# A recurrent attention kernel gets a new order of its slots: scores three slots and values four slots behind the projection, LayerNorm and FFN spread over more slots

## The reference

```python
xn = layernorm(x)
s = linear_attention_and_convolution(xn)                    # once
y = xn
for layer in range(6):
    q, k, v = split(shift(y) @ Wqkv)          # 16 heads of 64, 1024 columns each
    q = rotary(l2norm(q) * qs); k = rotary(l2norm(k) * ksc)
    sim = q @ k.T * 8      # each window of 32 tokens sees itself and the window before
    y = softmax(mask(sim)) @ v @ Wo + y
    a, gate = split(layernorm(shift(y)) @ W1 + b1)          # 341 columns each
    y = (a * gelu(gate)) @ W2 + b2 + y
out = x + s * silu(y)
```

## Time and profile before

| | us |
|---|---|
| median of 3 runs | 1839.14 (1838.91 to 1840.05) |
| the profiled execution, its own time | 1847.78 |
| its span, first to last instruction | 1846.0 |
| TensorE busy | 1697.0 (92%) |
| VectorE busy | 1422.5 (77%) |
| ScalarE busy | 1343.9 (73%) |
| GpSimd busy | 1307.7 (71%) |
| the 16 transfer engines, share of their span | 11.9% |

### The profile page before, as it was taken

One profiled execution on the slowest core, in us unless ns is written; L12 is line 12 of the kernel. 1 busy time (PEld: TensorE's weight loads), 2 busy tenths in 40 slices (PEclk: granted clock), 3 DMA queues, 4 the chain that ended last, 5 costly groups with the idle time before them and its releaser, 6 DMA issues.

```text
span 1846.0 us, 68784 instructions
## 1 busy us (share of the span) xinstructions
PE 1697.0 (92%) x26160; PEld 1292.7 (70%) x26160; DVE 1422.5 (77%) x3011; ACT 1343.9 (73%) x2663; POOL 1307.7 (71%) x1305
## 2 busy tenths in 40 slices
PE   6889999999999999999999999999999999999984
PEld 5667777777677777767777777777777777677763
DVE  4488777787887778788777777878778787787763
ACT  3367777777777777777777777777777777777764
POOL 5187777777777777777777777777777777776654
PEclk8799999999999999999999999999999999999986
DMA  5011101011110111111011111111101001100000
GB/s 161 10 36 40 32 28 34 29 41 43 35 30 28 34 40 42 35 31 30 28 46 41 33 34 28 30 34 48 37 28 34 28 26 41 36 26 24 26 21 23
DMA packets 41407, 66.14 MB, mean 36 GB/s; under 512 B 7072, under 2 KB 16032, under 8 KB 41376
## 3 DMA queue, kind: packets, MB, share of 16 engines
q1 hardware_dynamic: 40224, 65.38, 11.9%
q10 hardware_dynamic: 1152, 0.34, 0.1%
HBM read 20.61 MB, written 1.05 MB: 12 GB/s over the span
## 4 chain that ended last, share of the span: by engine, by line
PE 69%; ACT 11%; issue 10%; DVE 8%; POOL 2%; ACTq 1%; DMA 0%; POOLq 0%; DVEq 0%
PE ps_a L536 11%; PE ps_qs L536 10%; PE ps_f L536 10%; PE ps_po L536 8%; PE ps_q L536 7%; PE ps_k L536 5%; PE ps_v L536 5%; PE ps_po L651 4%; PE ps_qs L642 3%; PE ps_tk L642 3%; DVE ssq L1273 2%; ACT p_bd L940 2%; DVE prob L1310 2%; ACT L1008 2%; ACT squares L946 2%
## 5 line engine op out<-in xcount | busy, mean ns | idle before, releaser
L425 POOL TENSOR_TENSOR qk<-qk,rnorm 128x512 f32<-128x512 f32 x384 | 393.2, 1045 | 298.5 <-DVE rnorm L1300 298.5
L417 POOL TENSOR_TENSOR qk<-qk,qk_rot 128x512 f32<-128x512 f32 x384 | 483.8, 1276 | 118.0 <-DVE qk_rot L1267 118.0
L1273 DVE TENSOR_REDUCE ssq<-squares 128x8 f32<-128x512 f32 x384 | 257.9, 681 | 71.0 <-ACT squares L946 58.1
L940 ACT COPY p_bd<-ps_po 64x512 f32<-64x512 f32 x380 | 219.0, 576 | 24.9 <-PE ps_po L651 22.5
L432 POOL TENSOR_TENSOR prob<-prob,row_inv 128x512 f32<-128x512 f32 x192 | 200.2, 1043 | 41.8 <-DVE row_inv L1319 41.8
L1316 DVE TENSOR_REDUCE row_sum<-prob 128x8 f32<-128x512 f32 x192 | 131.7, 686 | 119.8 <-ACT prob L1047 119.2
L536 PEld LDWEIGHTS ps_qs<-k_t,q_t 64*32 64x32 f32 x12224 | 178.8, 107 | 56.9 <-issue 56.9
L536 PE MATMUL ps_qs<-k_t,q_t 64*32 64x64 f32 x12224 | 209.7, 218 | 0.0
L1047 ACT ACTIVATE prob<-prob 128x512 f32<-128x512 f32 x190 | 120.0, 632 | 110.3 <-DVE prob L1310 107.0
L536 PEld LDWEIGHTS ps_po<-p_bd,v_back 128*64 128x64 f32 x3056 | 162.4, 138 | 48.0 <-issue 31.5
L536 PE MATMUL ps_po<-p_bd,v_back 128*64 128x64 f32 x3056 | 193.4, 225 | 1.1 <-ACT p_bd L940 1.0
(11 more groups left out here) (231 smaller groups left out, 4102.3 us busy)
## 6 DMA issues: line engine op xcount, KB each, us to landing
v_back<-v_own SPq DMA_DIRECT2D x192, 192.0 KB, 2.4
w_raw<-in_wqkv SPq DMA_DIRECT2D x48, 192.0 KB, 2.3
v_back<-v_own SPq DMA_DIRECT2D x96, 64.0 KB, 2.1
wo_sb<-in_wo SPq DMA_DIRECT2D x12, 256.0 KB, 3.1
w_sb<-in_w SPq DMA_DIRECT2D x6, 341.0 KB, 3.4
w_sb<-in_w SPq DMA_DIRECT2D x6, 192.0 KB, 2.6
x_in<-in_x SPq DMA_DIRECT2D x4, 256.0 KB, 5.2
out<-s_out SPq DMA_DIRECT2D x8, 128.0 KB, 1.9
```

The source lines that it names most:

```text
L417: nc.gpsimd.tensor_tensor(qk[:, s, i, :], qk[:, s, i, :], qk_rot[:, s, i, :], ALU.add).then_inc(added, 1)
L425: nc.gpsimd.tensor_tensor(heads(qk[:, s, i, :]), heads(qk[:, s, i, :]), rnorm[:, s, 8 * i:8 * i + 8].unsqueeze(2).to_broadcast([P, 8, HEAD ...
L940: return nc.scalar.copy(o, i)
L1273: V.tensor_reduce(ssq[:, s, 8 * i:8 * i + 8], heads(squares[:, s, OCTET * i:OCTET * i + OCTET]), AX, ALU.add).then_inc(ssq_done, 1)
```

## The change

A slot is put in a new order on every engine, and the stages are moved apart. TensorE now does: q projection of `u`, scores of `u-3`, transpose of the probabilities of `u-4`, k and v projections of `u`, both transposes of `u-2`, one share of the step's LayerNorm, FFN or output projection, and the values of `u-4`. The scores thus read copies that were made in the slot before. ScalarE squares straight out of PSUM before VectorE rotates (`squares_of` waits for the projection, `rotate` for the squares), and the next projection waits for `rotate` (`q_scaled`, `k_scaled`) in place of the squares. The norms of `u-1` are finished at the slot's beginning, and GpSimd normalises `u-1` ahead of its sum for `u`. `out_projection` moves a slot later, `ln_spread` and the three `ff_up` go to the four slots of step `n+3`, `ff_down` to slot 1 of step `n+4`, now into `ps_tk`, and there it waits for `k_turned` of the same slot. `x_mid` gets four buffers, `LAG` is 5, the loads of `wo`, `w1`, `w2` come one step later, and the drain is rewritten for four units in flight. The final SiLU stage of three batches starts inside the last body.

```diff
-LAG = 3
+LAG = 5
...
-        x_mid = sb("x_mid", [P, 2, PADDED])
+        x_mid = sb("x_mid", [P, 4, PADDED])
... GpSimd, body:
-                    if live(u - 3):
-                        divide(u - 3, (j - 3) % 2)
-                    if live(u):
-                        add_halves(u, j % 2)
...
-                    if j == 1 and live_batch(n - 3):
-                        ff_gate(n - 3)
+                    if j == 1 and live_batch(n - 4):
+                        ff_gate(n - 4)
...
-                    if live(u):
-                        normalise(u, j % 2)
+                    if live(u - 1):
+                        normalise(u - 1, (j - 1) % 2)
+                    if live(u - 3):
+                        divide(u - 3, (j - 3) % 2)
+                    add_halves(u, j % 2)
... TensorE:
-            def ff_down(m):
-                pe.wait_ge(xn_ready, m + 2)
-                down_into(ps_f, m)
+            def ff_down(u, m):
+
+                pe.wait_ge(k_turned, u + 1)
+                down_into(ps_tk, m)
... TensorE, body:
+                    project(n, j, 0, ps_q, q_scaled, q_done)
+                    if live(u - 3):
+                        scores(u - 3, (j - 3) % UNITS, (j - 3) % 2)
+                    if live(u - 4):
+                        turn_p(u - 4, j % 2)
+                    project(n, j, 1, ps_k, k_scaled, k_done)
...
+                    project(n, j, 2, ps_v, v_copied, v_done)
                     if live(u - 2):
+                        turn_qk(u - 2, 0, j % 2)
+                        if j == 2 and live_batch(n - 4):
+                            pe.wait_ge(x_ready, BATCHES + n - 3)
+                        turn_qk(u - 2, 1, j % 2)
+                    if j == 0:
+                        if live_batch(n - 2):
+                            out_projection(n - 2, 1)
+                        if live_batch(n - 3):
+                            ln_spread(n - 3, u)
+                    if j == 1:
+                        if live_batch(n - 2):
+                            ln_mean(n - 2)
+                        if live_batch(n - 3):
+                            ff_up(n - 3, 0)
+                        if live_batch(n - 4):
+                            ff_down(u - 2, n - 4)
+                    if j == 2:
+                        if live_batch(n - 2):
+                            ln_variance(n - 2)
+                        if live_batch(n - 3):
+                            ff_up(n - 3, 1)
+                    if j == 3:
+                        if live_batch(n - 3):
+                            ff_up(n - 3, 2)
+                        if live_batch(n - 1):
+                            out_projection(n - 1, 0)
+                    if live(u - 4):
+                        values(u - 4, n - 1, j, j % 2)
... ScalarE, squares_of:
-                act.wait_ge((q_scaled, k_scaled)[i], u + 1)
+                act.wait_ge((q_done, k_done)[i], u + 1)
... ScalarE, body:
+                    if live(u - 5):
+                        keep_attention(u - 5, *place(n, j, 5))
+                    if live(u - 1):
+                        keep_v(u - 1, *place(n, j, 1))
+                    squares_of(u, 0, j % 2)
+                    if j == 1 and live_batch(n - 4):
+                        load_exp()
+                    if live(u - 1):
+                        start_norms(u - 1, (j - 1) % 2)
+                    if j == 2 and live_batch(n - 2):
+                        ln_square(n - 2)
+                    if live(u - 4):
+                        keep_p(u - 4, j % 2)
+                    if live(u - 3):
+                        softmax_exp(u - 3, (j - 3) % 2)
+                    squares_of(u, 1, j % 2)
                     if live(u - 2):
+                        keep_turned_q(u - 2, j % 2)
+                        keep_turned_k(u - 2, (j - 2) % UNITS)
+                    if j >= 1 and live_batch(n - 3):
+                        ff_copy(n - 3, j - 1)
+                    if j == 0 and live_batch(n - 4):
+                        load_gelu()
+                        gelu(n - 4)
... VectorE, rotate:
-                dve.wait_ge(done, u + 1)
+                dve.wait_ge(squared, u + 1)
... VectorE, body:
+                    if j == 1 and live_batch(n - 2):
+                        after_attention(n - 2)
+                    if j == 1 and live_batch(n - 3):
+                        ln_normalise(n - 3)
+                    if j == 2 and live_batch(n - 2):
+                        ln_center(n - 2)
+                    if j == 2 and live_batch(n - 4):
+                        after_ff(n - 4)
+                    if j == 3 and live_batch(n - 2):
+                        ln_var(n - 2)
+                    if live(u - 3):
+                        softmax_shift(u - 3, (j - 3) % 2)
+                    if live(u - 1):
+                        newton(u - 1, (j - 1) % 2, u - 2)
+                    sum_squares(u, 0, j % 2)
+                    rotate(n, j, 0)
+                    if live(u - 3):
+                        sums(u - 3, (j - 3) % 2)
+                    rotate(n, j, 1)
+                    sum_squares(u, 1, j % 2)
...
+                    clamp_unit(u, j % 2)
```

More of the change, by code:

```diff
@@ L200, in live_batch, with place @@
             return not isinstance(m, int) or 0 <= m < STEPS
-        def normed(n, j):
-            return live(UNITS * n + j) or (j == 1 and live_batch(n - 2))
-        def norms_before(n, j):
-            u = UNITS * n + j
-            return u if live(u) else UNITS * STEPS + n - STEPS
+        def place(n, j, back):
+            return n + (j - back) // UNITS, (j - back) % UNITS
         def wait(eng, s, value):
@@ L851, in drain @@
-                up_into(ps_k, LAST - 1, 0)
-                pe.wait_ge(sub_done, b + 1)
+                pe.wait_ge(sub_done, b + 1)
+                scores(d, 3, 1, ps_qs)
+                ff_up(LAST - 2, 0)
+                pe.wait_ge(attn_copied, a + 1)
+                values(b, LAST, 1, 1)
+                ln_variance(LAST - 1)
+                ff_up(LAST - 2, 1)
+                turn_p(c, 0, ps_v)
+                ff_up(LAST - 2, 2)
+                values(c, LAST, 2, 0, ps_tk)
+                out_projection(LAST, 0)
@@ L1056, in keep_p_from @@
-            def keep_p_from(ps, u, s):
-                act.wait_ge(pt_done, u + 1)
-                for h in range(2):
-                    rows = slice(64 * h, 64 * h + 64)
-                    last = copy(p_bd[rows, s, :, h, :], ps[rows, :].rearrange("p (g q) -> p g q", q=WINDOW))
-                last.then_inc(p_turned, 1)
-            def attention_from(ps, u, tile):
-                act.wait_ge(o_done, u + 1)
-                copy(attn_t[:, PAIRS:2 * PAIRS, 1 + P * tile:1 + P * tile + P],
-                     ps[:].rearrange("p (c t) -> p c t", t=P)).then_inc(attn_copied, 1)
@@ L1360, in silu_invert @@
             def silu_invert(b):
-                e = silu_e[:, columns(b)]
+                e = silu_e(b)
                 dve.wait_ge(silu_exp, b + 1)
@@ L1464, in body, with drain @@
+                    if j == 3 and live_batch(n - 2):
+                        dve.wait_ge(var_ready, n - 1)
+                    clamp_unit(u, j % 2)
                     if isinstance(n, int) and n == 0 and j == 0:
                         bias_add()
+            def drain():
+                a, b, c, d = END - 4, END - 3, END - 2, END - 1
+                newton(d, 1, d)
+                softmax_shift(b, 1)
+                after_attention(LAST - 1)
+                sums(b, 1)
+                softmax_shift(c, 0, ps_q)
+                ln_normalise(LAST - 2)
+                dve.wait_ge(xn_ready, LAST - 1)
+                ln_center(LAST - 1)
+                softmax_shift(d, 1)
+                sums(c, 0)
+                sums(d, 1)
+                ln_var(LAST - 1)
+                dve.wait_ge(var_ready, LAST)
+                clamp(1)
+                silu_invert(0)
+                newton(END, 1, END)
+                ln_normalise(LAST - 1)
+                silu_invert(1)
+                silu_invert(2)
+                after_ff(LAST - 3, ps_v)
+                after_attention(LAST)
+                ln_center(LAST)
+                after_ff(LAST - 2, ps_k)
+                ln_var(LAST)
+                dve.wait_ge(var_ready, STEPS)
+                clamp(1)
+                newton(END + 1, 1, END)
+                after_ff(LAST - 1)
+                ln_normalise(LAST)
+                silu_invert(3)
+                silu_invert(4)
+                silu_invert(5)
+                silu_invert(6)
+                after_ff(LAST, ps_f)
+                silu_invert(7)
+                silu_last(7)
```

485 lines of the change are left out of this document (167 added, 318 removed).

## The result

The changed kernel takes 1766.6 us (median of four runs, 1763.62 to 1767.12); the kernel before, run beside it on the same chip, took 1839.6 us. The ratio is 0.9587, with a 95% interval of 0.9564 to 0.961. The forecast was 1788.0 us with a range of 1752 to 1830.

A forecast was written before the change was run, and what follows sets the result against it. TensorE, busy 92%, was taken to set the step, with waits in slot 1 alone. 44 x (34.8 - 35.70) = -40, start -11, end 0 took 1839.1 us to 1788 us, range 1752 to 1830.

The forecast's parts named there:

- case A: Whole kernel: a step falls from 35.70 to 34.8 us, time 1788 us, own range 1766 to 1812; chance 0.50.
- The bound of 34.1 us a step: Lowest step time allowed in the main forecast: entries at 0.25, returns at nothing, wait at 0.2 us.
- The three old waits of slot 1: TensorE's waits for the subtraction (0.46), the division (0.75) and the copy of turned k (0.88): 2.1 us a step removed.
- the one new wait: Slot 1: `ff_down` waits for ScalarE's copy of the turned k, 0.4 to 0.5 us a step.
- The floor of 32.1: TensorE's own work a step: 24.1 us for four slots plus 8.0 for output projection, FFN and LayerNorm.
- entries: Passages from full-array work into work on parts of the array: five a step, 0.25 to 0.35 each, 1.5 us together.
- return: Passage from work on parts of the array back to the full array: 0.12 us each, 0.6 for five a step.
- Start and end: Steps 0 to 3 would give -11 us; the drain would give 0, with ±4.
- Rival C: VectorE's chain, held by GpSimd, makes TensorE wait 0.4 twice a step: step 35.6, time 1824 us; chance 0.22.
- the clamp: Small VectorE instruction after the second sum of squares, held by GpSimd: median would rise from 280 to above 500 ns.
- Rival D: Passages around the scores cost 0.45 us more on each of four islands: step 36.6, time 1868 us; chance 0.10.
- Rival B: Copies overlap better, `ff_down` does not wait, passages are nearly free: step 33.7, time 1740 us; chance 0.12.

The follow-up runs named there:

- without tables: Kernel before with GELU replaced by the identity and the loop's table loads left out: 1785.72 us, ratio 0.9683; same on the changed kernel: 1748.28 us, ratio 0.9478.
- `ff_up` first: Changed kernel with each `ff_up` moved ahead of the transposes of q and k: 1761.98 us, ratio 0.9542.
- Both experiments against it: Changed kernel with the exponential's table load moved to slot 0 behind GELU: 1744.65 us; changed kernel with `ff_down` moved to slot 2: 1745.18 us.
- the squares at the place tried: Changed kernel with ScalarE squaring after VectorE's rotation, behind the copies, and projections waiting for the squares: 1848.58 us, ratio 1.0025.

## Why the prediction was right, point by point

**The direction and its mechanism held, the size was short.** The measured 1766.6 us are 21 below the forecast, at the lower edge of what case A gave itself (1766 to 1812). The bound of 34.1 us a step given for A is also added wrongly: its own terms, 32.1 + 1.25 + 0.24 + 0.2, make 33.8. The three old waits of slot 1 (2.1 us a step) are gone, the one new wait is where I put it, and no other took their place. Predicted slots were 8.9, 9.2, 7.5 and 9.1, measured are 8.62, 9.42, 7.41 and 8.88.

**The steady stretch gave 61 us, not 40.** Two terms of the sum were off. I had 34.4 us a step before waits; it is 34.33 - 0.66 = 33.67. The floor of 32.1 holds. What lies above it, read slot by slot, is 1.3 of entries (0.10 behind the transposes in slot 0, 0.22 behind the spread, 0.35, 0.37 and 0.29 behind the three `ff_up`), 0.09 of return behind the output projection, and 0.15 at the loop's head. I had 1.5, 0.6 and 0.24. The term that was off most is the return: I read 0.12 a time out of `ff_down` (1.46 against a scaled 1.34), and counted it behind the scores four times. But the 1.34 us for mask and scores were read up to the start of an `ff_up`, a full-array piece, so that a return behind the scores was in the floor already, whatever it costs:

```profile
712.47 1.10 PE L536 MATMUL ps_qs<-k_t,q_t 64*32 64x64 f32 x64
```

From there to the `ff_up` at 713.50 pass 1.03 us, and from the scores to the transposes in the changed kernel as much, 719.19 - 718.16 = 1.03.

The second error is that waiting did not stand in slot 1 alone. Slot 2 of the kernel before held about 0.3 us of it, the amount by which it becomes shorter without tables (9.37 to 9.05). That leaves 1.2 us a step for passages and head before, where 1.6 come after. The gain is thus made of waits: -2.1 - 0.3 + 0.66, and 0.4 more for passages, which is -1.4.

The Trainium skill, "TensorEngine Tiling (Array Packing)", section "Key Properties", says that a change of tiling mode drains TensorE. The rows agree that there is a price and show how small it is here: 0.10 us into tiled work behind transposes (642.13 - 641.60 = 0.53 for work of 0.43, in the rows with `ff_up` first), and 0.09 back out of the output projection in slot 0 (1.88 for work of 1.79).

**The new wait was 0.66, not 0.4 to 0.5.** I had TensorE at `ff_down` 6.2 us into the slot and the copy's end at 6.7; they came at 6.37 and 6.83. The rest is the handoff: the copy ended at 723.87, and `ff_down` started at 724.07, 0.20 later. Both experiments against it leave 0.1 to 0.2 of it standing and give the rest, about 0.5, so that it lies on the path.

**Start and end.** For steps 0 to 3 I had -11 and they gave -9: steps 1 to 3 took 93.0 us where I had 92.6, and step 0 gave 1.5 in place of 3. For the drain I had 0, and it gave -8.7 with more work in it (508 TensorE records against 374). What failed is that I compared the paths and took the same pace for both. The granted clock over the drain was 0.70 of 2.4 GHz before and 0.89 after, and TensorE was busy in 54% of it before and in 67% after. No run separates the shorter waits from the clock.

**The rivals.** Rival C (VectorE takes over) did not come true, but its condition is near: with TensorE relieved by 0.23 a slot, the transposes of q begin to wait for the subtraction. A kernel with one VectorE instruction more in each slot was meant to measure that margin, and there is no time of it, so how far VectorE is from setting the slot stays open. Of the clamp, I said that its median would pass 500 ns. It went from 280 to 471, just short of that, and the longest took 1.34 us, beside GpSimd:

```profile
708.22 1.33 DVE L1257 TENSOR_SCALAR ssq_c<-ssq 128x18 f32<-128x18 f32 x1
708.24 2.51 POOL L418 TENSOR_TENSOR qk<-qk,qk_rot 128x512 f32<-128x512 f32 x2
...
710.71 0.69 DVE L1277 TENSOR_REDUCE row_max<-ps_qs 128x8 f32<-128x512 f32 x1 [1.16 <-PE ps_qs L529]
```

It ends at 709.55, 0.03 behind the first of the two GpSimd instructions (1.28 us). In the whole trace 166 of 194 clamps take over 0.3 us, and each of them ends 0.03 to 0.04 behind an instruction of GpSimd. That agrees with the lock held for a whole instruction that the Trainium skill, "SBUF — State Buffer", section "Who interferes with whom", states. The delay is hidden, since VectorE then stands idle for the scores. The Newton steps average 182 to 192 ns and so are rarely held. Rival D fell with the returns. Rival B (1740 us) was near on the step before waits, 33.7, and wrong on the wait; with most of the wait gone the kernels reach 33.8.

**What I was right about without the right reason.** I wrote of the squares only as pieces in ScalarE's queue. In this order the gain hangs on them: in my walk ScalarE never waits for the rotations, and I did not ask what it would cost if it did. With the squares at the place tried, the answer is about 80 us.

## What to carry to other kernels

When stages are moved apart in a pipeline written by hand, price the change on the queue of every engine, and ask of each wait that is turned around what stands behind it: with the same early squares one order gained 4% and the other lost 13%. Take work from the busiest engine as a test of what bounds a kernel, since a busy share does not tell: the same 0.23 us a slot was worth 7 us before and about 25 after. A wait can also be shorter than what a profile marks: compare the start of an instruction with the end of what it waits for. Gains of single edits add up only while they leave each other's slack alone, so time the combination, and read the slot that disappoints.

## What the runs showed of the hardware that I had not expected

- Behind `ff_up` (4 matmuls of 256 columns, with 0.67 us of work) about 0.2 us are lost before transposes on the full array (0.86 from start to start) and about 0.3 before work on parts of it (0.96 to 1.04), but nothing before a projection (0.68).
- From the end of ScalarE's copy to the start of the matmul that waits for it: 0.20 us for `ff_down`, and 0.14 for the mask of the kernel before (its copy ran from 720.96 for 0.59, the mask stands in the earlier trace rows). From the end of VectorE's `xn` to `ff_down` in the kernel before: 0.18.
- One VectorE instruction of 18 columns took from 0.17 to 1.34 us in the changed kernel; the long ones ended with an instruction of GpSimd.
- After waits in slot 1 (the early squares in the old order), TensorE ran part of a stretch at 1.2 GHz: 64 score matmuls took 1.93 us in place of 1.03.
